# A recommender tower on one Trainium2 core: x0 gathered for 32 samples at a time from one joined table and turned by copies through DRAM, in place of TensorE transposes

## What is computed

```python
x0 = xk = stack([tbl_f[ids[:, f]] for f in range(39)], axis=1)   # [1024, 39, 16]
outs = []
for W in (f0, f1, f2):                 # W is [39 * g, 128]; g = 39, then 128, 128
    z = einsum('bfd,bgd->bfgd', x0, xk).reshape(b, 39 * g, 16)
    xk = einsum('bpd,pm->bmd', z, W)
    outs.append(xk)
z = sum(concatenate(outs, axis=1), axis=-1)
h = relu(concatenate([z, dense_ctx], axis=1) @ W_top1 + b_top1)
y = relu(h @ W_top2 + b_top2) @ W_top3
```

## Time and profile before

| | us |
|---|---|
| median of three runs | 1393.21 |
| the profiled execution, its own time | 1393.13 |
| its span in the profile | 1391.3 |
| PE busy | 1294.6 |
| POOL busy | 1038.3 |
| DVE busy | 978.5 |
| ACT busy | 760.4 |

### The profile page before, as it was taken

One profiled execution on the slowest core, in us unless ns is written; L12 is line 12 of the kernel. 1 busy time (PEld: TensorE's weight loads), 2 busy tenths in 40 slices (PEclk: granted clock), 3 DMA queues, 4 the chain that ended last, 5 costly groups with the idle time before them and its releaser, 6 DMA issues.

```text
span 1391.3 us, 25265 instructions
## 1 busy us (share of the span) xinstructions
PE 1294.6 (93%) x5629; PEld 971.1 (70%) x5629; DVE 978.5 (70%) x3241; ACT 760.4 (55%) x2434; POOL 1038.3 (75%) x921
## 2 busy tenths in 40 slices
PE   0179999998999999999999999999999999999999
PEld 0057777776778777877778767877778777877754
DVE  2068778687876878688876778687885878688720
ACT  2136565466655566466664566466664565566631
POOL 7648868788787878788787878878787876566530
PEclk9999999999999999999999999999999999999999
DMA  8131122011211112111211112111211111111000
GB/s 220 25 112 53 47 70 64 6 54 46 80 53 52 47 38 74 27 53 47 79 53 52 47 24 64 50 53 47 78 53 53 46 25 58 51 52 45 1 1 0
DMA packets 73417, 72.97 MB, mean 52 GB/s; under 512 B 32428, under 2 KB 44690, under 8 KB 72716
## 3 DMA queue, kind: packets, MB, share of 16 engines
q1 hardware_dynamic: 60600, 67.88, 16.5%
q0 software_dynamic: 9984, 2.58, 2.2%
q10 hardware_dynamic: 2720, 1.48, 0.4%
HBM read 10.15 MB, written 0.00 MB: 7 GB/s over the span
## 4 chain that ended last, share of the span: by engine, by line
PE 50%; POOL 14%; DVE 11%; issue 10%; DMA 6%; ACT 5%; SPq 3%; DVEq 1%; POOLq 0%; ACTq 0%
PE ps L469 10%; PE ps L473 10%; PE ps L470 10%; PE ps L448 9%; DVE terms L805 9%; POOL terms L364 6%; POOL x_in L341 5%; PE ps L493 5%; DMA x_cols<-x_cols 4%; ACT terms L667 3%; DVE prods L777 3%; PE ps L558 2%; PE ps L483 2%; POOL prods_low L218 2%; DMA x_first<-x_cols 1%
## 5 line engine op out<-in xcount | busy, mean ns | idle before, releaser
L805 DVE SCALAR_TENSOR_TENSOR terms<-ps,x_scal,terms 128x128 f32<-128x128 f32 x2944 | 811.6, 346 | 276.0 <-PE ps L473 149.3
L667 ACT ACTIVATE terms<-ps,x_scal 128x128 f32<-128x128 f32 x2048 | 585.8, 375 | 388.6 <-PE ps L473 342.1
L364 POOL TENSOR_TENSOR terms<-terms 128x1024 f32<-128x1024 f32 (+2 forms) x384 | 565.0, 1471 | 168.2 <-DVE terms L805 142.9
L469 PE MATMUL ps<-w_high,x_high 128*128 128x512 f32 (+1 forms) x1280 | 592.5, 463 | 24.3 <-DVE terms L805 18.6
L473 PE MATMUL ps<-w_high,x_low 128*128 128x512 f32 (+1 forms) x1280 | 499.7, 390 | 6.1 <-ACT x_cols L619 5.6
L470 PE MATMUL ps<-w_low,x_high 128*128 128x512 f32 (+1 forms) x1280 | 497.8, 389 | 0.0
L341 POOL DMA_INDIRECT x_in<-in_tbl,ids_now x312 | 298.9, 958 | 100.5 <-issue 84.6
L469 PEld LDWEIGHTS ps<-w_high,x_high 128*128 128x128 f32 x1280 | 241.4, 189 | 136.5 <-DVE terms L805 50.5
L470 PEld LDWEIGHTS ps<-w_low,x_high 128*128 128x128 f32 x1280 | 242.4, 189 | 71.0 <-issue 29.8
L473 PEld LDWEIGHTS ps<-w_high,x_low 128*128 128x128 f32 x1280 | 241.2, 188 | 60.2 <-ACT x_cols L619 8.2
L448 PE MATMUL ps<-prods,w 117*128 117x512 f32 x262 | 135.3, 601 | 8.6 <-DVE prods L777 8.6
(11 more groups left out here) (45 smaller groups left out, 455.0 us busy)
## 6 DMA issues: line engine op xcount, KB each, us to landing
prods<-x_cols SPq DMA_DIRECT2D x192, 234.0 KB
x_first<-x_cols SPq DMA_DIRECT2D x96, 78.0 KB
x_in<-in_tbl,ids_now POOLq DMA_INDIRECT x312
x_cols<-x_cols SPq DMA_DIRECT2D x14, 312.0 KB
x_diag<-x_scal SPq DMA_DIRECT2D x256, 9.8 KB, 1.9
s<-in_f SPq DMA_DIRECT2D x3, 832.0 KB, 13.2
wt<-in_W_top ACTq DMA_DIRECT2D x1, 768.0 KB, 8.0
wt<-in_W_top ACTq DMA_DIRECT2D x1, 512.0 KB, 9.3
```

What stands on the lines that cost most here:

```text
L364: nc.gpsimd.tensor_tensor(t[:, 0:n], t[:, 0:n], t[:, n:2 * n], ALU.add).then_inc(s_tree, 1)
L469: nc.tensor.matmul(y, x1_high[:, par, at:at + P], high, start=True, stop=False)
L667: op = nc.scalar.activation(terms[:, u % 2, FB * ACT_BANKS.index(q) + i, :], ps[:, (BANKS * u + q) % RING, i * G:(i + 1) * G], ACT.Copy, s ...
L805: nc.vector.scalar_tensor_tensor(out=acc, in0=y, scalar=x0, in1=acc, op0=ALU.mult, op1=ALU.add).then_inc(s_mac, 1)
```

## The change

All tables are joined to one on the host, one above the other, and `first_row` holds the first row of each. The ids are laid out anew: a row of `ids_now` is one of four tables and one of 32 samples, so that one indirect DMA fetches four tables' rows for 32 samples and ten fetch a group (the fortieth table is padding: row 0). POOL adds `ids_base` to the ids once per batch (`number_rows`) and gathers three groups ahead, into one of two buffers.

`put` writes a group's 1280 rows of 64 bytes to the DRAM scratch `x0_rows`, in the order table, sample; `load_cols` reads them back by four copies, of 39, 39, 39 and 6 rows of 2 KB, into `x0_cols`. That takes the place of the sixteen transposes, ACT's stores and the `repeat` copies. Group 1's trip is issued on ACT's queue, all others on SP's. `w2` and the weights of the perceptron are loaded by SP after the x0_diag copies of group 0 (`load_late`); PE waits for `w2` at the end of step 1 and for the others at the tail.

```diff
-GATHERED, SUMMED = 8, 10
-TURNS = ((9, 7), (10, 0), (10, 4), (10, 8))
+SAMPLES = P // GROUPS
+FOUR = P // SAMPLES
+FETCHES = -(-F // FOUR)
+AHEAD = 3
...
+def grouped_ids(ids, sizes):
+
+    padded = np.zeros((B, FETCHES * FOUR), ids.dtype)
+    padded[:, :F] = ids
+    base = np.zeros(FETCHES * FOUR, np.uint32)
+    base[1:F] = np.cumsum(sizes)[:F - 1]
+    grouped = padded.reshape(NBATCH, GROUPS, SAMPLES, FETCHES, FOUR).transpose(0, 4, 2, 1, 3)
+    base = np.broadcast_to(base.reshape(FETCHES, FOUR).T[:, None, None, :], (FOUR, SAMPLES, GROUPS, FETCHES))
+    return grouped.reshape(NBATCH, P, GROUPS * FETCHES), base.reshape(P, GROUPS * FETCHES)
...
-        ids_now = sb("ids_now", [P, F], U32)
-        x0_in = sb("x0_in", [P, F, D])
+        ids_now = sb("ids_now", [P, GROUPS * FETCHES], U32)
+        x0_in = sb("x0_in", [P, 2, FETCHES, D])
+        ids_base = sb("ids_base", [P, GROUPS * FETCHES], U32)
+        row_at = sb("row_at", [P, GROUPS * FETCHES], U32)
...
+        def put(queue, bt, j):
+
+            queue.wait_ge(s_gather[j % 2], (bt * (GROUPS // 2) + j // 2 + 1) * (16 * FETCHES))
+            queue.dma_start(rows[j % GROUPS].rearrange("(n p) d -> p n d", p=P), x0_in[:, j % 2, :, :]).then_inc(s_put, 16)
+
+        def load_cols(queue, gf, j):
+
+            g = j % GROUPS
+            queue.wait_ge(s_put, gf * 16 + 16)
+            source = rows[g].rearrange("(f b) d -> f (b d)", b=SAMPLES)
+            for i in range(SPT + 1):
+                n = min(F, CYCLIC - i * F)
+                queue.dma_start(x0_cols[i * F:i * F + n, g * GCOLS:(g + 1) * GCOLS], source[0:n, :]).then_inc(s_load, 16)
...
-            sp.dma_start(w2[:, :, :], f2.rearrange("(f g) m -> g f m", g=G)).then_inc(s_w2, 16)
-
             def load_ids(bt):
-                sp.wait_ge(s_gather, bt * (16 * F))
-                sp.dma_start(ids_now[:, :], ids[bass.ds(bt * BATCH, BATCH), :].bitcast(U32)) \
-                    .then_inc(s_ids, 16)
-
-            def repeat(cols, n):
-
-                for i in range(1, SPT + 1):
-                    rows = min(F, CYCLIC - i * F)
-                    sp.dma_start(x0_cols[i * F:i * F + rows, cols], x0_cols[0:rows, cols]).then_inc(s_cyc, 16)
-                sp.wait_ge(s_cyc, n * (16 * SPT))
+                sp.wait_ge(s_row, bt)
+                sp.dma_start(ids_now[:, :], ids[bt].bitcast(U32)).then_inc(s_ids, 16)
+
+            def load_late():
+
+                sp.dma_start(w2[:, :, :], f2.rearrange("(f g) m -> g f m", g=G)).then_inc(s_w2, 16)
+                sp.dma_start(wt1[:, :, :], w_top1[0:3 * P, :].rearrange("(k p) n -> p k n", p=P)).then_inc(s_top, 16)
+                sp.dma_start(wt1_dense[:, :], w_top1[3 * P:3 * P + DENSE, :]).then_inc(s_top, 16)
+                sp.dma_start(wt2[:, :, :], w_top2.rearrange("(k p) n -> p k n", p=P)).then_inc(s_top, 16)
+                sp.dma_start(wt3[:, :], w_top3[:, :]).then_inc(s_top, 16)
+                sp.dma_start(bt1[:, :], b_top1[:, :]).then_inc(s_top, 16)
+                sp.dma_start(bt2[:, :], b_top2[:, :]).then_inc(s_top, 16)
 
             def move_first(j):
...
                     sp.wait_ge(s_x1, gf)
-                if j % GROUPS == 0:
-                    move_first(j)
                 at = j % GROUPS * GCOLS
                 for k in range(1, KT):
                     sp.dma_start(prods[0:KR, k, :], x0_cols[k:k + KR, at:at + GCOLS]).then_inc(s_second[k - 1], 16)
-                if j == 0:
-                    sp.wait_ge(s_cols, 4)
-                    repeat(slice(GCOLS, BATCH * D), 2)
-                if j % GROUPS < GROUPS - 1:
-                    move_first(j + 1)
+
+            def next_cols(gf, j):
+
+                sp.wait_ge(s_load, gf * (16 * (SPT + 1)) + 16 * (SPT + 1))
+                move_first(j)
+
+            def feed(bt, j, more=True):
...
+
+                gf = bt * GROUPS + j
+                move(gf, j)
+                if more:
+                    put(sp, bt, j + 1)
+                move_diag(gf, j)
+                if more:
+                    load_cols(sp, gf + 1, j + 1)
+                    next_cols(gf + 1, j + 1)
 
             load_ids(1)
-            sp.wait_ge(s_cols, 1)
-            repeat(slice(0, GCOLS), 1)
+            put(sp, 0, 0)
+            load_cols(sp, 0, 0)
+            next_cols(0, 0)
             move(0, 0)
+            next_cols(1, 1)
+            move(1, 1)
             sp.wait_ge(s_ones, 1)
             sp.wait_ge(s_scal, 1)
             for b in range(TB):
-                rows = slice(b * D, (b + 1) * D)
-                sp.dma_start(x0_diag[rows, 0, :, b, 0:F], x0_scal[rows, 0, :, :]).then_inc(s_diag[0], 16)
-            with sp.Fori(0, NBATCH - 2) as bt:
-                for j in range(1, GROUPS):
-                    move(bt * GROUPS + j, j)
-                    move_diag(bt * GROUPS + j, j)
-                load_ids(bt + 2)
-                sp.wait_ge(s_cols, bt * 4 + 8)
-                repeat(slice(0, BATCH * D), bt + 3)
-                move(bt * GROUPS + GROUPS, GROUPS)
-                move_diag(bt * GROUPS + GROUPS, GROUPS)
-            for gf in range((NBATCH - 2) * GROUPS + 1, NGROUP):
-                if gf % GROUPS == 0:
-                    sp.wait_ge(s_cols, 4 * NBATCH)
-                    repeat(slice(0, BATCH * D), NBATCH + 1)
-                move(gf, gf % GROUPS or GROUPS)
-                move_diag(gf, gf % GROUPS or GROUPS)
+                rows_b = slice(b * D, (b + 1) * D)
+                sp.dma_start(x0_diag[rows_b, 0, :, b, 0:F], x0_scal[rows_b, 0, :, :]).then_inc(s_diag[0], 16)
+            load_late()
+            put(sp, 0, 2)
+            move_diag(1, 1)
+            load_cols(sp, 2, 2)
+            next_cols(2, 2)
+            for j in range(2, GROUPS + 1):
+                feed(0, j)
+            with sp.Fori(1, NBATCH - 1) as bt:
+                load_ids(bt + 1)
+                for j in range(1, GROUPS + 1):
+                    feed(bt, j)
```

POOL's list, and PE's, ACT's and the call:

```diff
-            def gather(f):
+            def number_rows():
+                pool.tensor_tensor(row_at[:, :], ids_now[:, :], ids_base[:, :], ALU.add).then_inc(s_row, 1)
+
+            def gather(j, n):
+
+                at = j % GROUPS * FETCHES + n
                 pool.indirect_dma_start(
-                    out=x0_in[:, f, :], out_offset=None, in_=tables[f],
-                    in_offset=bass.IndirectOffsetOnAxis(ap=ids_now[:, f:f + 1], axis=0),
-                ).then_inc(s_gather, 16)
+                    out=x0_in[:, j % 2, n, :], out_offset=None, in_=tables,
+                    in_offset=bass.IndirectOffsetOnAxis(ap=row_at[:, at:at + 1], axis=0),
+                ).then_inc(s_gather[j % 2], 16)
 
             def prologue():
-                pool.wait_ge(s_ids, 16)
-                for f in range(F):
-                    gather(f)
+                pool.wait_ge(s_ids, 32)
+                number_rows()
+                pool.wait_ge(s_row, 1)
+                for j in range(AHEAD):
+                    if j >= 2:
+                        pool.wait_ge(s_put, 16 * (j - 1))
+                    for n in range(FETCHES):
...
-            def share(done, n, steps):
-
-                left = F - done
-                return range(done + left * n // steps, done + left * (n + 1) // steps)
+            def gathers(u):
+
+                t = u % TILES
+                return range(FETCHES * t // TILES, FETCHES * (t + 1) // TILES)
 
             prologue()
-
-            pool.wait_ge(s_ids, 2 * 16)
-            pool.wait_ge(s_turn, 4)
-            ahead = 12
-            for f in range(ahead):
-                gather(f)
-            for u in range(SUMMED):
-                if u < GATHERED:
-                    for f in share(ahead, u, GATHERED):
-                        gather(f)
-                add_up(0, u)
-
-            with pool.Fori(0, NBATCH - 2) as bt:
-                pool.wait_ge(s_ids, (bt + 3) * 16)
-                pool.wait_ge(s_turn, bt * 4 + 8)
-                add_up(bt, SUMMED)
-                for n in range(1, STEPS):
-                    if n <= GATHERED + STEPS - SUMMED:
-                        for f in share(0, n - 1, GATHERED + STEPS - SUMMED):
-                            gather(f)
-                    add_up(bt, SUMMED + n)
-            for u in range(SUMMED, 2 * STEPS):
-                add_up(NBATCH - 2, u, u < 2 * STEPS - TILES)
+            with pool.Fori(0, NBATCH - 1) as bt:
+                for u in range(STEPS):
+                    if u == TILES:
+                        pool.wait_ge(s_ids, bt * 16 + 3 * 16)
+                        pool.wait_ge(s_gather[1], (bt * (GROUPS // 2) + GROUPS // 2) * (16 * FETCHES))
+                        number_rows()
+                        pool.wait_ge(s_row, bt + 2)
+                    if u % TILES == 0:
+                        pool.wait_ge(s_put, (bt * GROUPS + u // TILES + AHEAD - 1) * 16)
+                    add_up(bt, u)
+                    for n in gathers(u):
+                        gather(u // TILES + AHEAD, n)
```

(63 more changed lines are left out.)

52 lines of the change are left out of this document (18 added, 34 removed).

## The result

| | us |
|---|---|
| before, median of four runs | 1393.06 (1392.34 to 1393.88) |
| changed, median of four runs | 1343.69 (1343.38 to 1347.66) |
| ratio, 95% interval | 0.9652 (0.9633 to 0.9671) |
| the profiled execution of the changed kernel | 1347.66 |
| forecast | 1337.7 (1318 to 1361) |

The change makes the kernel 3.5% faster, 6.0 us less than forecast. The profiled execution is the slowest of the four, so the same kernel was profiled once more beside the experiments (label after_again: median 1343.32 of five runs; that profile's own time 1344.57, span 1342.8). Both profiles are read here.

A forecast was written before the change was run, and what follows sets the result against it. The prediction took PE, nearly gapless in the steady part, as the bound, with a head of idle PE before it. Sum: 1393.1 - 37.0 - 6 + 3 - 15.4 = 1337.7 us, range 1318 to 1361.

The forecast's parts named there:

- Head (1): Start of the kernel: the second layer's first matmul (S) comes at 43.1 us in place of 80.13, a gain of 37.0.
- nine distances of 1.33: Group 0's gathers: first at 4.1 us, then nine spacings of 1.33 us, so the tenth is issued at 16.1.
- Second factors (2): Soon after S: group 1's six factor copies go ahead of the x0_diag copies, removing PE's 5.07 us stop: -6 us.
- Costed at nothing: Group 1's DRAM trip, issued by ACT, which waits for the put: covered by ACT's idle time, 0 us.
- the case of a late trip: If group 1's DRAM trip took over 9 us, x1's store would be late by the rest.
- Late weights (3): End of step 1: PE waits for f2, loaded behind the x0_diag copies: +3 us, bounds 0 and 7.6.
- Batch (4): Steady part: transposes and the wait for x0_cols leave PE, -2.2 us at each of seven batch borders, -15.4 in all.
- POOL (5): Steady part: POOL needs 149.6 us per batch against 154.6 left; even spread relieves, new wait burdens: counted as nothing.
- the 7 us: Sign of a wrong forecast: ACT's waits for POOL rise above 7 us a batch.
- SP's queue (6): Steady part: loads and x0_first add 8.6 us behind x0_diag, of 19.9 us available, so they stay hidden.
- D: Rival: the way through DRAM, with 64 B pieces, paces every group; slower than before, up to 1431 us; chance 0.03.
- E: Rival: something else holds S where it was, so no head gain, 1375 us; chance 0.02 with all nearer no change.

The follow-up runs named there:

- e7: The changed kernel with f2 and the perceptron's weights loaded at the head, on the queues and in the order of the kernel before: 1342.03 us, ratio 0.9634.
- e4: The changed kernel with group 1's second factors put back behind the x0_diag copies of group 0: 1345.27 us, ratio 0.9650.
- e1: The changed kernel with PE's wait for f2 moved from the end of step 1 to the third layer's first matmul: 1339.95 us, ratio 0.9614.
- e5: The changed kernel with the first addition of POOL's tree left out: 1322.77 us, ratio 0.9491.
- e6: The kernel before the change with the first addition of POOL's tree left out: 1376.23 us, ratio 0.9879.
- e2: The changed kernel with the row numbering in two parts, the last group's four steps after the other three: 1339.05 us, ratio 0.9605.
- e3: The changed kernel with DVE's split of f1's low part held back until group 0's gathers have landed: 1340.81 us, ratio 0.9622.
- e8: The changed kernel with e1, e2 and e3 together, and the late weights loaded behind group 2's x0_first: 1329.68 us, ratio 0.9540.
- e9: e8 with the third low part of each next group's products made by DVE instead of POOL: 1325.05 us, ratio 0.9505.
- e10: The changed kernel with only the third low part of each next group's products made by DVE instead of POOL: 1338.94 us, ratio 0.9609.

## Why the prediction came out as it did

**Head (1): right in sum, by two errors that cancel.** S was forecast at 43.1 and came at 43.4 and 45.2. The step that failed is "nine distances of 1.33": that mean of 38 gathers spreads a few slow ones thin, and in the changed kernel four of them (1.83, 2.63, 2.59 and 2.54 us) stand in the first ten. The tenth was issued at 21.75 in the first profile in place of 16.1, and at 17.04 in the second. Before, only one of the first ten was slow (1.45 us), because the three long subtractions ran from 17.00 to 25.27, behind them. The change brought them forward to 13.00: with f2 and the perceptron's weights out of the way f1 lands earlier. So the late weights put the subtractions beside group 0's gathers; in e7, with the weights early, the tenth is issued at 15.63. The rows of before held the hint: the subtraction L826 was read for f1's low part, and not set beside the gathers. In turn the put took 2.4 us where 4.7 was taken, and lies below the lower bound of 2.9; the loads took 3.0 to 3.1 where 4.6 was taken. The upper bound had priced each of the put's 1280 packets at the queue's mean of 61 ns; in the trace they take 9 ns each. The Trainium skill ("DMA: Bandwidth & Descriptors", Anatomy of one DMA) has a fit, made for DMAs that GpSimd issues, by which the put is estimated at 2.2 us; the trace supports it with 2.4; the dearer price that its Specifications suggested for pieces under 512 B does not show at this size. Behind the first weights alone group 0's put was cheap; behind f2 (e7) it took 4.7.

**Second factors (2): the gain was real and then lost.** In e7, without a stop for f2, S to first sum is 9.5 us shorter than before, where the forecast's -6 and one batch's -2.2 make 8.2. In the changed kernel the medians of e4 and after_again put the order at some 2 us. "Costed at nothing" for ACT's trip was wrong by 2.0 us in after_again: PE had ended x1 at 39.90 (43.39 - 3.49), ACT issued the loads until 40.91 (39.22 + 1.69), and the split of x1 starts at 41.92. The loads in ACT's list account for half of the 2.0; the other half has no releaser in the trace. The forecast had named this as the case of a late trip; here the trip starts later than thought (put at 36.79, 11.0 us after x0_first(0), where 5.0 was taken), since POOL's second ten gathers had to land first, and no step of the forecast counted those for group 1.

**Late weights (3): the stop was forecast, the clock behind it was not.** The stop was forecast at 3 and is 3.78 in one profile and 7.28 in the other; e1 prices it at 3.4 net, with an S 2.5 later beside it. x0_first(2) at 80.86 did not hold up PE. What no step had is the clock: in the second profile PE's granted clock is 0.65 from 70 to 75 us, behind the stop, against 1.00 from 60 to 65, ahead of it, so a stop costs more than its length. The kernel before had shown it: its stop of 5.07 us up to 92.73 was followed by a granted clock of 0.50 from 92 to 98 us, which the forecast did not read. And e7 shows that the alternative, a later S without a stop, comes to the same.

**Batch (4) and POOL (5): the step that failed.** "Nothing" for POOL was wrong. The transposes were worth 2.9 us a batch (e5 against e6), 2.2 forecast; POOL took back 1.75, of which the numbering is 1.0 (e2). Net 1.15 a quiet batch instead of 2.2, and the period is 155.65 instead of 154.6. The argument was that POOL ends 5 us under the batch. But POOL's slack over a batch does not help: ACT's first bank of a step waits for x2 of two steps earlier, so it is the stretch of single steps that decides. The costs were right: a group of four steps takes 36.8 us on POOL (from 419.43 to 456.21 us), 36.7 forecast. But 149.6 us of work in 155.7 left room only as an average; POOL paused for no more than the 1.5 us at the numbering from 406 us, the step ahead of it, to 538, and ACT's waits passed the 7 us that had been set as the sign of a wrong forecast. That six batches together still came within 1.0 us of the forecast is luck. The longer periods make up for it: 4.0 and 2.9 us before, with a pause of POOL at a gather in each (4.26 us at 324.54, no releaser recorded), and 1.8 in the changed kernel (2.19 us at 821.80). No step had the 5.1 us between them.

**SP's queue (6): right.** ACT waits for no first factor in the steady part, and D and E are out: the way through DRAM paces nothing, and S did move.

**What is left.** Of the 6.9 us between the forecast's span and the second profile's, 6.0 lie between S and the first sum. There the gain of (2) went into the stop for f2 and half the clock behind it, which by e1's profile take up to 7.5 us where the forecast had 3; the late start of ACT's first scaling has a part that no run measures.

**Open.** That ACT starts late (L663 5.1 us after S in after_again, 1.2 in the first profile and in e7) has no releaser in the trace, or a matmul that had ended long before; in all of e1 to e5 and e8 to e10 it is 4.0 to 6.9 us. In some of them the split of x1 before it is late in the same way: once x1 is summed and ACT's loads are issued, it starts 0.05 us later in the first profile and in e3, but 1.0 in after_again, 2.3 in e2 and 3.8 in e1. No run isolates it, and it was not tried to move ACT's put and loads behind its split of x1. Why gathers and subtractions fell differently in two executions of one kernel (24.14 or 20.26 for the put) is open too: the first gather starts at 4.54 us in one and 3.97 in the other, the first long subtraction at 13.00 and 12.78, and no run moves one against the other.

## What to carry to other kernels

A mean over a long row of equal instructions is no price for the first ten: look at those that count, at what runs beside them on the other engines, and at what the change itself moves beside them. When an engine is paced step by step through short buffers, compare it with the step, not with the batch, and settle what it costs by halving its work in both kernels. A stop that comes later can eat what is gained before it, so remove the last wait first.
